# Local transformer of a four-stage kernel: three sequences under way instead of two, PSUM banks by function, a new order on every engine, and the next layer's weights loaded in parts

## The reference, cut to what matters

```python
for i in range(DEPTH):                                     # DEPTH = 6
    x = attn_layer(shift_tokens(x), Wqkv[i], q_scale[i], k_scale[i], Wo[i]) + x
    x = ffn_layer(shift_tokens(x), ln_g[i], ln_b[i], W1[i], b1[i], W2[i], b2[i]) + x
...
def attn_layer(x, Wqkv, qs, ksc, Wo):
    q, k, v = jnp.split(x @ Wqkv, 3, -1)                   # 16 heads of 64 each
    q = l2norm(q) * qs
    k = l2norm(k) * ksc
    q = q * cos * scale + rotate_half(q) * sin * scale     # and k with 1 / scale
    out = local_attention(q, k, v)                         # softmax over own and previous window
    return out @ Wo
def ffn_layer(x, g, bln, W1, b1, W2, b2):
    a, gate = jnp.split((layernorm(x) * g + bln) @ W1 + b1, 2, -1)
    return a * jax.nn.gelu(gate) @ W2 + b2
```

## Time and profile before

| | |
|---|---|
| time, three runs | 2866.08, 2872.39, 2876.25 us; median 2872.39 |
| the profiled execution | 2870.65 us; its span 2868.8 us, 1.85 us lie around it |
| busy over the span | PE 2667.4 us, DVE 1976.4, ACT 1771.4, POOL 1305.5 |
| mean granted clock | 0.979 of full speed |
| the local transformer | from 143.0 us (first `tokens`) to 2077.9 us (last `second_residual`) |

### The profile page before, as it was taken

How to read it: one execution, slowest core, us unless ns; L and a number is a source line. 1 busy time by engine, 2 the same in 40 slices (tenths; PEclk the granted TensorE clock), 3 DMA queues, 4 the chain that set the end, 5 groups by cost and what they waited for, 6 DMA issues and landing times.

```text
span 2868.8 us, 103417 instructions
## 1 busy us (share of the span) xinstructions
PE 2667.4 (93%) x41474; PEld 1961.0 (68%) x41474; DVE 1976.4 (69%) x4817; ACT 1771.4 (62%) x3791; POOL 1305.5 (46%) x1725
## 2 busy tenths in 40 slices
PE   7689999999999999999999999999889988899898
PEld 5556666666666666666666666666677877799767
DVE  6767776777767776777777777777656777555565
ACT  5567666776767766776776766767644336433365
POOL 5554554455454554455455454554433116300373
PEclk9999999999999999999999999999999989999999
DMA  2100001000010001000010000000000200000022
GB/s 81 66 13 15 11 15 52 16 14 12 16 52 15 11 15 52 16 14 12 16 52 15 15 11 17 15 11 15 12 5 4 79 1 7 3 1 0 3 71 83
DMA packets 51095, 66.71 MB, mean 23 GB/s; under 512 B 24521, under 2 KB 30356, under 8 KB 49428
## 3 DMA queue, kind: packets, MB, share of 16 engines
q1 hardware_dynamic: 50964, 64.87, 8.1%
HBM read 38.23 MB, written 1.05 MB: 14 GB/s over the span
## 4 chain that ended last, share of the span: by engine, by line
PE 51%; DVE 21%; POOL 13%; issue 9%; ACT 5%; POOLq 1%; DVEq 1%; SPq 0%; DMA 0%; ACTq 0%
PE ps L853 6%; POOL area L1574 6%; PE ps L814 5%; DVE area L2069 4%; POOL area L1568 4%; DVE area L2037 4%; PE ps L775 4%; DVE area L2039 4%; PE ps L781 4%; PE ps L956 3%; PE ps L940 3%; PE ps L941 3%; PE ps L880 2%; PE ps L846 2%; DVE ssq L2023 2%
## 5 line engine op out<-in xcount | busy, mean ns | idle before, releaser
L1132 ACT ACTIVATE area<-ps 64x128 f32<-64x128 f32 (+4 forms) x1520 | 769.8, 532 | 446.5 <-PE ps L781 131.0
L1568 POOL TENSOR_TENSOR area<-area 128x512 f32<-128x512 f32 x384 | 489.0, 1274 | 817.8 <-DVE area L2039 817.8
L1574 POOL TENSOR_TENSOR area<-area,rnq 128x512 f32<-128x512 f32 x384 | 396.9, 1044 | 14.4 <-ACT rnq L1266 0.6
L775 PE MATMUL ps<-lw,area 128*128 128x512 f32 x768 | 399.6, 623 | 0.7 <-ACT area L1132 0.7
L2023 DVE TENSOR_REDUCE ssq<-area 128x8 f32<-128x512 f32 x384 | 261.3, 681 | 35.9 <-ACT area L1248 24.5
L2095 DVE SCALAR_TENSOR_TENSOR area<-ps,lcol,area 128x128 f32<-128x128 f32 (+1 forms) x288 | 82.9, 343 | 276.2 <-ACT area L1289 272.2
L781 PE MATMUL ps<-ident,area 128*128 128x128 f32 x1536 | 241.8, 280 | 33.5 <-POOL area L1574 32.0
L2039 DVE TENSOR_TENSOR area<-ps,table 128x512 f32<-128x512 f32 x384 | 261.0, 680 | 0.0
L2037 DVE TENSOR_TENSOR area<-ps,table 128x512 f32<-128x512 f32 x384 | 259.6, 676 | 0.4 <-issue 0.4
L1248 ACT ACTIVATE area<-ps 128x512 f32<-128x512 f32 x384 | 227.3, 592 | 43.6 <-PE ps L775 43.6
L781 PEld LDWEIGHTS ps<-ident,area 128*128 128x128 f32 x1536 | 171.4, 144 | 75.2 <-POOL area L1574 73.6
(11 more groups left out here) (304 smaller groups left out, 5744.7 us busy)
## 6 DMA issues: line engine op xcount, KB each, us to landing
lvm<-area SPq DMA_DIRECT2D x384, 65.0 KB, 2.0
lw<-in_wqkv SPq DMA_DIRECT2D x6, 1536.0 KB
area<-in_moe_w SPq DMA_DIRECT2D x24, 256.0 KB, 2.7
lw<-in_wout SPq DMA_DIRECT2D x6, 512.0 KB
ctxT<-in_ctxT SPq DMA_DIRECT2D x64, 38.5 KB, 1.8
lw<-in_moe_w SPq DMA_DIRECT2D x8, 256.0 KB, 2.8
lw<-in_wff SPq DMA_DIRECT2D x6, 341.0 KB
lw<-in_moe_g SPq DMA_DIRECT2D x1, 1152.0 KB
```

Of the source, the lines that this page charges most:

```text
L775: nc.tensor.matmul(ps[s][:, j, :], xsT[s], wqkv[w.p][:, j * 512:(j + 1) * 512], start=True, stop=True).then_inc(l_qk_ps, 1)
L1132: return nc.scalar.activation(dst, src, ACT.Identity if kw else ACT.Copy, **kw)
L1568: pool.tensor_tensor(QR[s][:, cols], QR[s][:, cols], RA[s][:, cols], ALU.add).then_inc(l_rsum, 1)
L1574: pool.tensor_tensor(rows, rows, rnq[s][:, 8 * j:8 * j + 8, None].to_broadcast([S, 8, LD]), ALU.mult).then_inc(l_qkn, 1)
```

## The change

Each engine's `halves(a, b)` becomes `stages(a, b, c)`: three items are under way, `a` at its queries and keys, `b` at its transposes, scores and softmax, `c` at its projection and feed-forward part. The arithmetic and the number of matmuls, activations and vector instructions per item stay. PSUM banks no longer belong to a sequence: each function has a bank or a pair of banks, whatever the item, and so some instructions now wait until another item's instruction has read the bank. In SBUF there are still two sets of buffers, one for items of even and one for items of odd number.

The weights of a layer come in 12 parts with 15 transfers. They are issued one part behind each of the items 2 to 13 of the layer before, behind that item's `middle_values`.

```diff
-        ps = [ctx.enter_context(nc.psum_tensor(f"ps{s}", [128, 4, 512], F32)) for s in range(G)]
+        banks = ctx.enter_context(nc.psum_tensor("ps", [128, 8, 512], F32))
+        ps = [banks[:, 4 * s:4 * s + 4, :] for s in range(G)]
+        lb_tokens, lb_qk, lb_qkT, lb_v = 7, (6, 3, 0, 3), (5, 2, 0, 2), (5, 6)
+        lb_scores, lb_probs, lb_pv = ((5, 6), (0, 1)), (1, 4), ((0, 1), (6, 7))
+        lb_outputs = (1, 4)
+        lb_project, lb_shift, lb_xnT, lb_up, lb_down = 6, 4, 1, (7, 4), 2
...
-        def local_transformer(engine, halves, prepare=None, done=None):
-            def layer(p, lp, last, last_pair=False):
+        def local_transformer(engine, stages, prepare=None):
+            def layer(p, lp, last):
+                q, lq = 1 - p, lp + p
                 with engine.Fori(0, IT - 1) as pr:
-                    halves((1, At(p, lp, pr)), (0, At(p, lp, pr)))
-                    halves((0, At(p, lp, pr + 1)), (1, At(p, lp, pr)))
-                ahead = None if last else (0, At(1 - p, lp + p, 0))
+                    stages((0, At(p, lp, pr + 1)), (1, At(p, lp, pr)), (0, At(p, lp, pr)))
+                    stages((1, At(p, lp, pr + 1)), (0, At(p, lp, pr + 1)), (1, At(p, lp, pr)))
                 if prepare and not last:
-                    prepare(1 - p, lp + p)
-                halves((1, At(p, lp, IT - 1)), (0, At(p, lp, IT - 1)))
-                halves(ahead, (1, At(p, lp, IT - 1)))
-                if done and not last_pair:
-                    done(p, lp)
+                    prepare(q, lq)
+                stages(None if last else (0, At(q, lq, 0)), (1, At(p, lp, IT - 1)), (0, At(p, lp, IT - 1)))
+                stages(None if last else (1, At(q, lq, 0)), None if last else (0, At(q, lq, 0)), (1, At(p, lp, IT - 1)))
 
             if prepare:
                 prepare(0, 0)
-            halves((0, At(0, 0, 0)), None)
+            stages((0, At(0, 0, 0)), None, None)
+            stages((1, At(0, 0, 0)), (0, At(0, 0, 0)), None)
             with engine.Fori(0, DEPTH // 2 - 1) as lp:
                 for p in range(2):
                     layer(p, lp, False)
             for p in range(2):
-                layer(p, DEPTH // 2 - 1, p == 1, True)
+                layer(p, DEPTH // 2 - 1, p == 1)
...
+                rows = dram["wqkv"][l, :, :]
+                parts = [[(wqkv[p][:, at:at + 512], rows[:, at:at + 512])] for at in range(0, 3 * INNER, 512)]
+                parts += [[(wout[p][:, c:c + 4, :], dram["wout"][l, :, c:c + 4, :])] for c in (0, 4)]
...
+                return parts
...
-            def middle_values(s, w):
-                sp.wait_ge(l_v, nth(0, w.it, s, 2, 1))
+            def middle_values(s, unit):
+                sp.wait_ge(l_v, (unit + 1) * 2)
                 for odd in range(2):
                     at = 64 * odd
                     sp.dma_start(LVM[s][at:at + 32, :, :], LV[s][at:at + 32, 1, :, :]).then_inc(l_vm, 16)
                     sp.dma_start(LVM[s][at + 32:at + 64, :, :], LV[s][at + 32:at + 64, 0, :, :]).then_inc(l_vm, 16)
 
-            def halves(a, b):
-                if a: middle_values(*a)
-            def next_weights(p, lp):
-                sp.wait_ge(ffn_done, G + (lp * 2 + p + 1) * B)
-                load_layer(p, lp * 2 + p + 2)
-            local_transformer(sp, halves, done=next_weights)
+            def layer(l):
+                with sp.Fori(0, IT) as pr:
+                    for s in range(G):
+                        middle_values(s, l * B + pr * G + s)
+            def layer_and_next_weights(l, p):
+                parts = layer_parts(p, l + 1)
+                for n in range(B):
+                    middle_values(n % G, l * B + n)
+                    if n == 2:
+                        sp.wait_ge(ffn_done, G + l * B)
+                    if 2 <= n < 2 + len(parts):
+                        for dst, src in parts[n - 2]:
+                            sp.dma_start(dst, src).then_inc(lw_loaded[p], 16)
+            layer(0)
+            with sp.Fori(0, DEPTH // 2 - 1) as lp:
+                layer_and_next_weights(lp * 2 + 1, 0)
+                layer_and_next_weights(lp * 2 + 2, 1)
+            layer(DEPTH - 1)
...
             def queries_keys(s, w, j):
                 if j == 2:
-                    pe.wait_ge(lw_loaded[w.p], 144 * (w.lp + 1))
+                    pe.wait_ge(lw_loaded[w.p], 240 * (w.lp + 1))
+                if j == 0:
+                    follow(pe, l_v, nth(0, w.it, s, 2, 1) - 2)
+                if j == 1:
+                    pe.wait_ge(l_rb, nth(0, w.it, s, 4, 1))
+                if j == 2:
                     pe.wait_ge(l_xsT, nth(0, w.it, s))
-                nc.tensor.matmul(ps[s][:, j, :], xsT[s], wqkv[w.p][:, j * 512:(j + 1) * 512],
+                nc.tensor.matmul(banks[:, lb_qk[j], :], xsT[s], wqkv[w.p][:, j * 512:(j + 1) * 512],
                                  start=True, stop=True).then_inc(l_qk_ps, 1)
...
             def values(s, w, j):
-                pe.wait_ge(l_qkT, nth(0, w.it, s, 4, keys_first(2 + j)))
+                if j == 1:
+                    pe.wait_ge(l_shift, nth(0, w.it, s, 2, 0))
                 heads = wqkv[w.p][:, K2:K2 + INNER].rearrange("p (c k e) -> p c k e", k=2, e=LD)
                 for odd in range(2):
-                    last = nc.tensor.matmul(ps[s][64 * odd:64 * odd + 64, 2 + j, :].rearrange("p (c e) -> p c e", e=LD),
+                    last = nc.tensor.matmul(banks[64 * odd:64 * odd + 64, lb_v[j], :].rearrange("p (c e) -> p c e", e=LD),
                                             xsT[s][:, 64 * j:64 * j + 64], heads[:, :, odd, :], start=True, stop=True)
                 last.then_inc(l_v_ps, 1)
...
-            def scores(s, w, m):
+            def scores(s, w, m, near=None):
 
                 if m == 0:
-                    pe.wait_ge(l_qkT, nth(0, w.it, s, 4, keys_first(1)))
-                else:
-                    pe.wait_ge(l_v, nth(0, w.it, s, 2, 1))
+                    pe.wait_ge(l_qkT, nth(0, w.it, s, 4, 1))
+                if m == 1:
+                    if near:
+                        pe.wait_ge(l_rb, nth(0, near[1].it, near[0], 4, 0))
+                    pe.wait_ge(l_qkT, nth(0, w.it, s, 4, 3))
...
-            def probs_values(s, w, m):
-                pe.compute_val(nth(0, w.it, s, 2, m))
-                pe.compute_val(64 * nth(0, w.it, s))
-                pe.wait_ge(consts_cast, 2)
-                pe.wait_ge(l_vm, 64 * nth(0, w.it, s))
-                pe.wait_ge(l_pT, nth(0, w.it, s, 2, m))
+            def probs_values(s, w, m, near=None):
+                if m == 0:
+                    pe.compute_val(nth(0, w.it, s, 2, 0))
+                    pe.compute_val(64 * nth(0, w.it, s))
+                    pe.wait_ge(w1_loaded, 160)
+                    pe.wait_ge(l_pT, nth(0, w.it, s, 2, 0))
+                    pe.wait_ge(l_vm, 64 * nth(0, w.it, s))
+                if m == 1:
+                    pe.compute_val(nth(0, w.it, s, 2, 1))
+                    if near:
+                        pe.compute_val(nth(0, near[1].it, near[0], 4, 2))
+                    pe.wait_ge(w1_loaded, 160)
+                    if near:
+                        pe.wait_ge(l_rb, nth(0, near[1].it, near[0], 4, 2))
+                    pe.wait_ge(l_pT, nth(0, w.it, s, 2, 1))
...
+            def stages(a, b, c):
+                if c: outputs_T(*c, 0)
+                if b: queries_keys_T(*b, 2)
+                if c:
+                    outputs_T(*c, 1)
+                    project(*c, 0)
+                    project(*c, 1)
+                if b:
+                    queries_keys_T(*b, 0)
+                    queries_keys_T(*b, 3)
+                if c: shift_back(*c)
                 if a: tokens_T(*a)
+                if b: scores(*b, 0)
                 if a: queries_keys(*a, 2)
+                if c: normed_T(*c)
+                if a: queries_keys(*a, 3)
+                if b: queries_keys_T(*b, 1)
+                if c:
+                    up(*c, 0)
+                    up(*c, 1)
+                if b:
+                    scores(*b, 1, a)
+                    values(*b, 1)
                 if a:
+                    values(*a, 0)
                     queries_keys(*a, 0)
                 if b:
+                    probs_T(*b, 0)
                     probs_T(*b, 1)
                 if a: queries_keys(*a, 1)
                 if b:
+                    probs_values(*b, 0)
+                    probs_values(*b, 1, a)
+                if c:
+                    down(*c, 0)
+                    down(*c, 1)
+                    down(*c, 2)
...
             def values(s, w, j):
-                act.wait_ge(l_v_ps, nth(0, w.it, s, 2, j))
-                copy(LV[s][:, j, :, 0:LD], ps[s][:, 2 + j, :].rearrange("p (c e) -> p c e", e=LD)).then_inc(l_v, 1)
+                if j == 0:
+                    follow(act, l_vm, 64 * nth(0, w.it, s) - 64)
+                if j == 1:
+                    act.wait_ge(l_v_ps, nth(0, w.it, s, 2, 1))
```

(61 more changed lines are left out.)

361 lines of the change are left out of this document (184 added, 177 removed).

## The result

The changed kernel takes 2766.02 us (median of 4 runs, 2765.13 to 2766.13), the one before 2871.26 in the same comparison: a ratio of 0.963, 95% interval 0.9615 to 0.9646. The forecast was 2855 with a range of 2815 to 2895: the sign was right, the size too small by 89 us. The profiled execution has a span of 2763.3 us against 2868.8.

What follows compares the result with a forecast made beforehand. PE was taken as the bound (busy 306 of 320 us). A call of 18.5 + 0.85 + 0.1 = 19.45 us against 19.55 gave -9 over 94 calls, layer ends -8: 2870.65 to 2853.6, as median 2855, range 2815 to 2895.

Steps and rivals of the forecast that it cites:

- PE's work: PE's matmuls and transposes per call, without waits: taken as 18.5 us, bounds 18.4 and 18.8.
- The waits that go: PE's old waits at outputs_T, queries_keys, after up and at normed_T: all 0.89 us per item counted as gone.
- the wait that comes: PE at an item's first probs_values, for the DMA copies of middle_values: chain 4.64 us, cover 3.79, so 0.85 per call.
- Waits of 0.89: PE's idle or longer-than-twin time per item before the change: 0.89 us waiting, the other 18.66 us work.
- This is all that a better order can win in the steady part: Ceiling for reordering PE's steady items: some 94 items by 0.89 us, 84 us or 2.9% of the time.
- Small waits 0.1: PE behind DVE's second half of outputs and at normed_T: 0.1 us per call together, bounds 0 and 0.5.
- Layer ends -8.4: Two PE gaps inside probs_values, read as instructions late behind weight transfers, go with weights in parts: -8.4 us, bounds -12.6 and 0.
- Start and drain 0, bounds 8: Two calls short at the start, two more at the end: taken as 0, bounds 8 us either way.
- Before's call 19.55: One item on PE before the change, start to start from 1023.57 to 1043.12: 19.55 us, used as baseline.
- C (a shared bank): Rival: b's second scores wait until DVE rotated a's first keys in bank 0, 3.1 us against 3.2; 2902 us, chance 0.22.
- B: Rival: PE's work at its lower bound plus only DMA waits, call 19.25 or less; 2832 us, chance 0.19.
- The rule under B: Skill's advice to use all eight PSUM banks, read as removing all repeating gaps; call not below 18.4, 2755 us, chance 0.04.

## Why the prediction was wrong

The step that failed is the term of PE's work, **"so I take 18.5; bounds 18.4 and 18.8"**, and behind it "That makes 0.89 us of waits and 18.66 us of work per item". It measured 17.5. The waits that go and the wait that comes were named rightly; what was off is the size of PE's work, and with it of the waits, by 1.0 us a call, 94 us in all.

- *Waits of 0.89.* I took as waiting what a row showed idle or what a twin was longer by, and as work all the rest, 0.47 to 0.59 for four transposes "by what follows them". What followed them was, by the PEld rows, a late input; a run shows it at `up` and at `outputs_T`, for the rest it is argued. In the changed kernel their length is 0.44, `up`'s 1.33, `shift_back`'s 0.39. If 17.5 was PE's work before too, the waits were some 2 us a call (19.70 less 17.5, the loop's branch included), of which 0.9 could be seen. The signs stood in the trace: the PEld waits above, and in the earlier trace rows a 0.66 for four transposes beside a 0.60.
- *"This is all that a better order can win in the steady part: some 94 items by 0.89 are 84 us."* The steady part won 108 while a new wait of 1.03 was added.
- *The new wait.* Right in place, kind and links: 0.62 from ACT's start to the first issue, 1.83 to the fourth, 2.0 to land. It is 1.07 in the mean, not 0.85: the chain from `values` is 4.64 as reckoned, with 0.18 more from landing to PE, and the cover is 3.72 for my 3.79 (1.10 in the call shown).
- *Small waits 0.1.* Now 0.05, ahead of `normed_T`.
- *Layer ends -8.4.* The two gaps of 4 us in straight code went, the one at the jump back stayed, and shorter ones came. Start and layer ends together gave 6.4. The term took the gaps at their length and left out the lower clock behind them: the two calls were 13 us longer than their neighbours. Alone the weights in parts are worth 12 by the medians and 6.5 by the spans, in the changed kernel 1.5 to 6.6, not clear of noise: that 8.4 comes near is partly luck.
- *Start and drain 0, bounds 8.* The drain is 7 us longer, inside the bound.
- *Before's call 19.55.* That was one item; the mean is 19.70 for the branch in every second call. This put 0.15 x 94 = 14 us less into my gain than there was.
- *Rivals.* C (a shared bank) didn't come: PE waits neither at the second `scores` nor at the first `values`. B's direction was right and its floor too high by the same term. C's 3.1 us was also added up too high: the parts it names give 2.9. The rule under B, that more banks remove the repeating gaps, came nearer than the sum did: of the old waits only `normed_T`'s is left. No run parts the banks from the order, though, and the Trainium skill has such gaps in "Perfetto Trace Analysis", "Optimization Strategy", as what a lack of PSUM or SBUF can cause, not as its sure sign.
- *Sum.* 2855 - 84 (a call of 18.56 for 19.45) - 14 (before's call) + 7 (drain) + 2 (layer ends) = 2766.

## What to carry to other kernels

A PE row's end is modelled, so a group's length from start to start contains waits that no idle figure shows, 0.16 us behind each group of transposes here and more when its loads run late. Before costing "work", take each group's shortest length in any context and the waits of the weight loads, and ask which inputs PE comes to sooner than their answer can be there; relieving the engines gave 0.9% here, another item's work in between, with banks by function, 3.7%. When a wait for a transfer stands in every call, first shorten the chain that leads to it (here one issue moved to another queue, 59 us); work moved over the wait may have been covering another link of the same ring.

## What was not expected of the hardware

A copy of 0.23 us on VectorE took 1.08 when it started just behind the start of a GpSimd product of 1.04 us, with one input or two, and 0.29 as a one-input reduction; three edits that moved PE's list by some tenths of a microsecond brought it in. Sixteen products onto the same 32 output partitions took 1.03 us placed together, and all 64 of the four windows 1.53 when mixed. Behind a gap of 4.14 us PE went on at a granted clock of 0.50. A reached wait ahead of a group on PE costs 0.011 us.
